# Turning the second feed-forward weight by a sign matrix: one full float32 product, or two products of a float32r high and low part

## What is computed

```python
hidden = jax.nn.silu(up_gate) * up_lin
hidden = fwht(hidden)                      # butterflies over 2048, times 1/sqrt(2048)
out = jnp.einsum('bsh,dh->bsd', hidden, W2)
```

## Time and profile before

| | before |
|---|---|
| time, median of 3 runs | 3085.48 us (3082.89 to 3085.62) |
| the profiled execution's own time | 3086.84 us |
| its span | 3084.5 us |
| granted TensorE clock, mean | 0.996 of full speed |
| PE, DVE, ACT, POOL busy | 99%, 61%, 50%, 46% of the span |
| `fold_mult` L521, 32 matmul instructions | 592 ns each, in four groups of 8 |
| `project_qkv` and what precedes it | the first 356 us |

### The profile page before, as it was taken

How to read it: one execution, slowest core, us unless ns; L and a number is a source line. 1 busy time by engine, 2 the same in 40 slices (tenths; PEclk the granted TensorE clock), 3 DMA queues, 4 the chain that set the end, 5 groups by cost and what they waited for, 6 DMA issues and landing times. The chain is left out here.

```text
span 3084.5 us, 41512 instructions
## 1 busy us (share of the span) xinstructions
PE 3049.4 (99%) x15536; PEld 2097.8 (68%) x15536; DVE 1885.7 (61%) x3186; ACT 1529.3 (50%) x2880; POOL 1430.3 (46%) x497
## 2 busy tenths in 40 slices
PE   7999999999999999999999999999999999999999
PEld 5788755555555555555555554788888888888887
DVE  5445988888888888888888874743332323323222
ACT  4333366667766666676666666743222222222221
POOL 2223388888888888888888885000000000000000
PEclk9999999999999999999999999999999999999999
DMA  7665588888888888888888876942211212111111
GB/s 261 198 202 181 157 172 180 182 175 181 180 185 181 177 182 179 183 183 181 181 175 183 182 157 170 309 159 92 72 48 58 69 38 76 45 61 60 45 62 34
DMA packets 149653, 446.91 MB, mean 145 GB/s; under 512 B 26960, under 2 KB 44624, under 8 KB 114256
## 3 DMA queue, kind: packets, MB, share of 16 engines
q0 software_dynamic: 32288, 211.83, 33.5%
q1 hardware_dynamic: 116112, 232.43, 25.4%
q10 hardware_dynamic: 1056, 0.00, 0.0%
HBM read 167.37 MB, written 80.21 MB: 80 GB/s over the span
## 5 line engine op out<-in xcount | busy, mean ns | idle before, releaser
L1268 DVE TENSOR_REDUCE mxp<-pmax 128x1 f32<-128x512 f32 x1968 | 1202.3, 680 | 243.9 <-PE pmax L1046 243.9
L1217 ACT ACTIVATE prob<-pexp 128x512 f32<-128x512 f32 x2023 | 1020.5, 625 | 398.5 <-PE pexp L1095 396.1
L1046 PE MATMUL pmax<-k,q 96*128 96x512 f32 x1968 | 811.2, 412 | 1.1 <-PEq L432 1.1
L1095 PE MATMUL pexp<-q,k 98*128 98x512 f32 x2023 | 803.2, 399 | 0.6 <-ACT prob L1217 0.6
L53 PE MATMUL pproj<-h2f,w 128*128 128x512 f32 x3072 | 717.6, 389 | 0.0
L53 PEld LDWEIGHTS pproj<-h2f,w 128*128 128x128 f32 x3072 | 576.8, 188 | 119.5
L1344 POOL TENSOR_TENSOR gsum<-gsum,prob 128x2048 f32<-128x2048 f32 x127 | 583.5, 4595 | 37.2 <-ACT prob L1217 26.6
L1046 PEld LDWEIGHTS pmax<-k,q 96*128 96x128 f32 x1968 | 373.6, 190 | 280.2 <-DVE mxp L1268 169.7
L1989 POOL TENSOR_TENSOR x2f<-sil,x2f 128x512 f32<-128x512 f32 x1 | 1.3, 1282 | 1085.6 <-DVE sil L1974 1085.6
L1106 PE MATMUL pctx<-prob,v 128*32 128x512 f32 x4096 | 493.4, 598 | 0.0
L1921 DVE TENSOR_TENSOR hid<-sil,pproj 128x512 f32<-128x512 f32 x128 | 88.1, 688 | 630.7 <-PE pproj L53 629.2
(11 more groups left out here) (147 smaller groups left out, 1759.1 us busy)
## 6 DMA issues: line engine op xcount, KB each, us to landing
gsum<-prob POOLq DMA_DIRECT2D x187, 1024.0 KB, 7.4
w<-w_scratch SPq DMA_DIRECT2D x128, 256.0 KB, 2.6
q<-q_scratch SPq DMA_DIRECT2D x96, 256.0 KB, 4.6
k<-k_scratch SPq DMA_DIRECT2D x96, 256.0 KB, 6.2
q_scratch<-obq SPq DMA_DIRECT2D x32, 512.0 KB, 5.3
k_scratch<-obq SPq DMA_DIRECT2D x32, 512.0 KB, 3.7
xin<-in_L_attn_query_dram SPq DMA_DIRECT2D x8, 1024.0 KB, 8.7
v_scratch<-vst SPq DMA_DIRECT2D x8, 1024.0 KB, 5.2
```

What stands on the lines that cost most here:

```text
L1046: pe.matmul(pmax[:, bank, :], qst[slot][0:KR, qt * P:(qt + 1) * P], kst[slot][0:KR, kc * TOK:(kc + 1) * TOK], start=True, stop=True).then_ ...
L1095: pe.matmul(score_bank(g, n), kst[slot_of(g)][:, kt * P:(kt + 1) * P], qst[slot_of(g)][:, j * TOK:(j + 1) * TOK], start=True, stop=True).t ...
L1217: act.activation(prob_tile(g, kt)[:, j * TOK:(j + 1) * TOK], score_bank(g, n), ACT.Exp, scale=SCALE).then_inc(exp_done, 1)
L1268: dve.tensor_reduce(mxp[:, par, u // QJ, u % QJ:u % QJ + 1], pmax[:, bank, :], X, ALU.max).then_inc(mx_done, 1)
```

## The change

The sign product takes a float32r high part and a float32r low part instead of the float32 block. `fold_take` writes the high part into the place of `w2t`, a new DVE step `fold_low` writes the low part into the place of `full`, and `fold_mult` adds two products in PSUM. The sign matrix, whose entries are 1 and -1, is copied once by ACT to a float32r tile `signs`. The buffer `full` is now written also by `fold_low`: `fold_low` waits until DVE's lows of the next tile have read it, and `low_parts`, which writes it next, waits until PE has done the earlier sign products.

```diff
+        with ExitStack() as halves:
+            w2_low_half = halves.enter_context(nc.sbuf_tensor("w2_low_half", [P, HID], F32R))
         full = sb("full", [P, DC, TOK])
...
+        with ExitStack() as halves:
+            w2_high_half = halves.enter_context(nc.sbuf_tensor("w2_high_half", [P, HID], F32R))
         wt = sb("w2t", [P, HID])
+        signs = sb("signs", [P, P], F32R)
...
                 def fold_mult(t):
                     n = FOLD_AT.index(t)
-                    pe.wait_ge(keep["had_in"], 16)
+                    pe.wait_ge(signs_set, 1)
                     for i in range(DC):
                         pe.wait_ge(w2_taken, DC * n + i + 1)
-                        pe.matmul(pt[:, i, :], had[:, :], wt[:, i * D:(i + 1) * D], start=True, stop=True).then_inc(w2_mm, 1)
+                        pe.wait_ge(w2_lowered, DC * n + i + 1)
+                        pe.matmul(pt[:, i, :], signs[:, :], w2_high_half[:, i * D:(i + 1) * D], start=True, stop=False)
+                        pe.matmul(pt[:, i, :], signs[:, :], w2_low_half[:, i * D:(i + 1) * D], start=False,
+                                  stop=True).then_inc(w2_mm, 1)
...
                 def fold_take(t):
-                    if n:
+                    if n == 0:
+                        act.wait_ge(keep["had_in"], 16)
+                        act.activation(signs[:, :], had[:, :], ACT.Copy).then_inc(signs_set, 1)
+                    else:
                         act.wait_ge(w2_out, 16 * n)
...
-                        act.activation(wt[:, i * D:(i + 1) * D], pt[:, i, :], ACT.Copy).then_inc(w2_taken, 1)
+                        act.activation(w2_high_half[:, i * D:(i + 1) * D], pt[:, i, :], ACT.Copy).then_inc(w2_taken, 1)
...
                 def low_parts(t):
+                    folded = len([f for f in FOLD_AT if f < t - 1])
+                    if folded:
+                        dve.wait_ge(w2_mm, DC * folded)
...
+                        if j == FOLD_TURN and t in FOLD_AT:
+                            fold_low(t)
...
+                def fold_low(t):
+                    n = FOLD_AT.index(t)
+                    dve.wait_ge(h_lo, DC * (t + 2))
+                    for i in range(DC):
+                        dve.wait_ge(w2_taken, DC * n + i + 1)
+                        dve.tensor_tensor(w2_low_half[:, i * D:(i + 1) * D], pt[:, i, :],
+                                          w2_high_half[:, i * D:(i + 1) * D], ALU.subtract).then_inc(w2_lowered, 1)
```

More of the change, by code:

```diff
@@ L405, in project_qkv @@
         w2_taken = sem("a_w2_taken")
+        w2_lowered = sem("a_w2_lowered")
         w2_mm = sem("a_w2_mm")
+        signs_set = sem("a_signs_set")
         w2_scaled = sem("a_w2_scaled")
```

## The result

The changed kernel takes 3087.7 us (median of 22 runs, 3083.04 to 3091.49), the kernel before in the same rounds 3084.01 us (22 runs, 3079.07 to 3089.11). The ratio is 1.0013, with a 95% interval of 1.0008 to 1.0019: slower by 3.7 us, where 4.7 us less were forecast.

A forecast was written before the change was run, and what follows sets the result against it. PE, busy 99% of the span, was taken to set the pace, with DVE and POOL just behind. Tiles 1, 3, 5 and 6 give 1.1 + 1.2 + 0.8 + 1.6 = 4.7 us: 3080.8 us, range 3077.6 to 3085.5.

The forecast's parts named there:

- PE's saving: On PE, a block's eight sign-product passes fall from 3.44 to 1.82 us: 1.62 us per block, 6.5 in four.
- The cover over the subtractions: On DVE, a block's four subtractions end near 72.7 us, with 3.3 us of cover left, costing PE nothing.
- POOL's lead, "0.8 us sooner": Behind each product, closer DVE scalings let the block's store and next butterflies come 0.8 us sooner, not 1.62.
- landed no sooner: Worst case: the block's store, started 0.8 us sooner, lands no sooner; 2.3 us saved in all, 3083.1 us.
- The lows: On DVE, lows get in only between butterflies; one more fits in tile 1, which gives 1.1 us; tile 3 gives 1.2.
- My slower rival: The sign product waits 5.8 us for subtractions held by butterflies: 3102 us; chance 0.08, smaller slips elsewhere included.
- smaller slips elsewhere: Other slips costing over 6 us, such as an attention falling worse with its DMAs; included in a chance of 0.08.
- the part behind the attention's start is unchanged in length: Outside `project_qkv`, the rest keeps its length; an attention differing by over 2 us would show the forecast wrong.
- The sign that I gave for tile 5: In tile 5, PE's wait for POOL grows from about 0.8 to 1.6 us; no growth would mean POOL kept up.

The follow-up runs named there:

- quiet: The kernel before and the changed kernel, each with a separate butterfly buffer and butterflies held until the next tile's statistics are done: 3081.79 and 3076.46 us.
- vlate: The kernel before and the changed kernel, each with the value store issued behind the next tile's first four query stores: 3082.52 and 3077.71 us.
- low_only: The kernel before with the four DVE subtractions per block added, their result unread, and the float32 products kept: 3084.51 us, ratio 1.0002.
- rep_before: The kernel before, unchanged, timed and profiled once more: 3084.1 us, ratio 0.9998.
- rep_after: The changed kernel, unchanged, timed and profiled once more: 3088.03 us, ratio 1.0013 to the kernel before.
- high_twice: The changed kernel without the DVE subtractions, the sign matrix multiplied twice with the high part: 3087.53 us, ratio 1.0011 to the kernel before.
- again_1: The changed kernel, unchanged, one more profile: one run, 3085.11 us.
- again_3: The changed kernel, unchanged, the last of three more profiles: one run, 3091.44 us.
- fill: The changed kernel with eight unread matmuls (1.8 us) in each of three places where PE waits: 3084.84 us, ratio 1.0000 to the kernel before.
- quiet_before: The kernel before with a separate butterfly buffer and the butterflies held until DVE finished the next tile's statistics: 3081.79 us, ratio 0.9988.
- ping_after: The changed kernel with a separate buffer for the butterflies, so they don't wait for the store to land: 3081.27 us, ratio 0.9994 to the kernel before.

## Why the prediction was wrong

- **PE's saving: right.** 1.82 us for eight passes, 1.62 saved per block; the two pairs quiet and vlate give 6.6 us in the stretch.
- **The cover over the subtractions: right.** low_only is at 1.0002; in the changed kernel they end at 73.2, forecast as 72.7, and PE comes at 76.4.
- **POOL's lead, "0.8 us sooner": the step that failed.** The scalings do end and the store is issued sooner, by 1.0 us (0.8 from their closer steps, and 0.2 since the first starts sooner). But I let the landing follow the issue, and took as the worst case a store that "landed no sooner". Averaged over three profiles with the old products (before, rep_before, low_only) the butterflies start at 13.0, 12.8 and 12.3 us in the frame, and over six with the new ones (changed, rep_after, high_twice, again_1 to again_3) at 13.6, 13.7 and 12.7. The term that was +0.8 us per tile is -0.7, -0.9 and -0.4. My bound was made from the spread of three landings of the same schedule, and the schedule was what changed (its sum is also off by 0.1: 3085.48 - 2.3 is 3083.2, not 3083.1). The runs showed in its place a landing that goes with that of SP's token load, 1.6 to 4.2 us behind it, and a token load that lands 1.0, 1.2 and 0.4 us later with the new products; I had set no price on what is shared with SP's transfers.
- **The lows: right in kind.** They count in gaps between butterflies as forecast: in tile 1 they end 1.15 us behind the last one, with one more inside. With the late butterflies the waits became 2.7, 2.4 and 2.4 us from where PE is ready, to 0.6, 0 and 0.8 before: 6.1 us more of waiting for 6.5 us saved. Of the forecast 4.7 us, 0.4 were left.
- **What is in no step: the clock.** I priced a wait of PE at its own length. Here a wait of 1.9 us or more was in some executions followed by 3.4 us at half clock, 1.7 us more. One to three of these turned the 0.4 us into a loss of 1.2 to 4.9 us in the profiles (281.2 to 284.9, against 279.9 for the mean of the two profiles of before), and the medians' 3.7 us lie within that.
- **The rivals.** My slower rival was one on the subtractions, and it did not happen; "smaller slips elsewhere" was not worked out. That the part behind the attention's start is unchanged in length was right (2726.2 and 2725.0 us, for 2727.9 and 2725.7). The sign that I gave for tile 5, a wait grown to 1.6 us, came out as 2.4.

## What to carry to other kernels

A faster instruction on the bounding engine is worth its saving only where the next engine behind it has slack, and two short waits of 0.5 us in the trace were already the sign that this one had none. Where that next engine waits for a DMA, don't let the landing follow the issue: look at what else is on the DMAs at that time, and price a later landing too. Here a wait of TensorE of some 2 us cost more than its length in a share of the executions, so a change that gathers saved time into a wait can lose. With the transfers or the buffer moved that make the wait, the whole saving arrived in the stretch, and the kernel was 0.22 to 0.26% faster than before. An edit that moves one transfer can move others in the same queue: look at all of them before the effect is put down to one.

## What the runs showed of the hardware

- A 1 MB store issued by POOL landed 6.9 us behind the end of its issue on average (6.2 to 7.6) with a value store and a token load of SP on the DMAs, 7.9 to 9.3 us when it was issued 1.0 us sooner into them, and 4.1 to 4.7 us with neither. With them, its first packet moved 7.8 to 9.6 us into the frame, after the value store had landed, and it landed 1.6 to 4.2 us behind the token load, even where that was issued after it.
- Half clock behind a pause of PE: in the three places of tiles 1, 3 and 5 never with waits of 1.8 us or less (the longest were 1.73 in fill and 1.77 in again_1); with waits of 1.9 to 2.7 us it came in some executions and not in others, and its length was 3.4 us each time. All 18 profiles have a pause of PE of 1.1 us at the attention's start; quiet_before's was followed by half clock (0.65 from 358 to 360 us, 0.50 to 362), the others were not, so the length of the pause alone doesn't decide.
- Two DVE instructions of four columns, one of them with a single SBUF input, took 1.1 and 2.0 us beside POOL's butterflies (ping_after), against 0.17 and 0.16 us without them.
